# One program block for all stages, with the shared network's opening placed inside the last sequence's attention

## The chip, the cores and the metric

One NeuronCore of a Trainium2 chip runs the whole kernel. The metric is device microseconds (us) of one execution. Engines are named as in the profile: PE is TensorE (PEld its weight loads), DVE is VectorE, ACT is ScalarE, POOL is GpSimd, SP is SyncE, which only issues DMAs here.

## The reference, cut to what matters

The input x has 16 sequences of 512 tokens with 256 features. Two layers run one after the other:

```python
x = x + layernorm(attention(layernorm(x)))
x = x + layernorm(ffn(layernorm(x)))
```

The attention has 16 heads of 16 features and a causal window of 128 tokens, a small attention over 64 pooled latents, a sigmoid gate that mixes the two, and an output projection. The ffn is a mixture of experts: a router picks 2 of 8 experts (256 to 352 to 256) for each of the 8192 tokens, and a shared network (256 to 704 to 256, silu(gate) times up, then down) is applied to every token; the two are added. All matrix products are in fp32, made of three products of fp32r parts (a high part, and a low part that is the value less its high part).

## The kernel before

The work is four stages, each in a `nc.Block()` of its own (lines 317, 1496, 1910, 2170). At a block's end all five engines meet at a barrier before the next one starts. Inside a block each engine has its own hand-written order, and semaphores alone tie the engines together.

**Attention** (L317 to L1290). 16 sequences go through a software pipeline. An iteration `body(i)` has 16 positions `u`; in it run the scores, exps, selects and weighings of sequence i, the projections of i+1 (`nxt`), the norm of i+2 (`after`), the gate, mixing and output projection of i-1 (`prev`), and the residual and second norm of i-2 (`before`). Iterations 14 to 17 are unrolled; in 16 and 17 no scores are left, only the tail of sequences 14 and 15: `gate_in` (L886), `gate_mix` (L905), POOL's `mix` (L474), PE's `turn_mix` (L1193), `project_out` (L1029 to L1031, L1205), `att_stats` (L922), `residual_add` (L932), `normed` (L524). The normed rows of each sequence are stored in DRAM (`store_xn2`, L357). PE's last weighing of values is L1084.

**Shared network and routing, first half** (L1496 to L1893). It starts with `wait_ge(stored, 32 * SEQS)` on every engine: the last sequence's rows have to be in DRAM. Rounds m = 0 to 7 each take a pair of sequences: item "b" (sequence 8 + m) is only routed, item "a" (sequence m) is routed and goes through the shared network. SP loads the rows (L1509) and the weights (L1523), which ACT and DVE split into high and low parts (L1618, L1778). PE turns rows (`turn_rows`, L1816), ACT copies them (L1602, L1610), DVE makes the low part (`rows_low`, L1724), PE makes the router's logits (L1833). DVE picks the two experts (`take_logits` L1678, `choose_first` L1666 to L1685, `choose_second` L1666 to L1699), PE ranks the rows within each expert (`ranks`, L1843), DVE turns the ranks into row numbers (`place`, L1707 to L1715), and POOL scatters the rows to the experts' regions (L1562, 8 indirect DMAs an item). Meanwhile PE runs six chunks n of `gate_up` (L1394 to L1396, 12 matmuls each, 512 columns) and six of `shared_down` (12 matmuls of 256 columns). POOL also splits the experts' weights, a chunk at a time (`split_chunk`, L1569, L1571), which SP loads into one staging buffer. At the end POOL writes zero rows behind every expert's rows (L1583).

**Experts** (L1910 to L2160): 136 blocks of 128 rows, in loops. Every engine first waits in `first_part_over` for all scatters.

**Shared network, second half, and the last layer norm** (L2170 to L2454): sequences 8 to 15 through the shared network, while POOL gathers the experts' results (L2226). SP, POOL, ACT and DVE wait in `second_part_over` for the last blocks' stores.

The tensors in SBUF are allocated per stage, so the stages share the memory: the second stage's tensors lie over the attention's, which is why it could not start earlier.

Of the kernel before, what the change touches and what calls it, by code (L numbers as in the profile page):

```python
# [3 lines left out]

# [113 lines left out]
def sandwich_kernel(nc, x, qkv_w, qkv_b, rq_w, rq_b, rkv_w, rkv_b, rout_w, rout_b, out_w, out_b, gl_w, gr_w,  # L118
# [4 lines left out]
    P = 128  # L123
# [28 lines left out]
    with ExitStack() as ctx:  # L152
# [8 lines left out]

        attention = ExitStack()
        with attention:
# [3 lines left out]

            wqk_h = sb("wqk_h", [P, 2, C, D], f32r)
# [28 lines left out]
            x_in = sb("x_in", [P, T, D])  # L197
            x_res = sb("x_res", [P, T, D])
            xT_h = sb("xT_h", [P, C, S], f32r)
            xT_l = sb("xT_l", [P, C, S], f32r)  # L200
            qk_h = sb("qk_h", [P, 2, S], f32r)
            qk_l = sb("qk_l", [P, 2, S], f32r)
            kS = sb("kS", [P, 2, HEADS // 2, S], f32r)
            qS = sb("qS", [P, 2, HEADS // 2, S], f32r)
            v_sb = sb("v_sb", [P, 2, T, HEADS, PAD])
            row_max = sb("row_max", [P, G, HG, T])
            maxT = sb("maxT", [HG * T, G, P], f32r)
            prob = sb("prob", [P, SLOTS, HG, WIN])
# [72 lines left out]

            units = [(g, b) for g in range(G) for b in range(T)]
# [34 lines left out]
            with nc.Block() as block:  # L317

                @block.sync
                def _(sp):  # L320
                    sp.wait_ge(zeroed, 2)
                    with nc.allow_non_contiguous_dma(reason="512 biases, once"):
                        for dst, src in loads:
                            sp.dma_start(dst, src).then_inc(weights_in, 16)

                    sp.wait_ge(split, 1)

                    def load_x(i):
                        if not isinstance(i, int) or i > 0:
                            sp.wait_ge(*front.filled(i - 1, "xT1"))  # L330
                        sp.dma_start(x_in[:, :, :], x[i].rearrange("(t p) d -> p t d", p=P)).then_inc(x_loaded, 16)

                    def spread_heads(i, buf, half):
                        if half == 0 and (not isinstance(i, int) or i > 1):
                            for hp in range(2):
                                sp.wait_ge(*keyed.all_filled(i - 1, f"T0{hp}"))
                        tiles = slice(half * HEADS // 4, (half + 1) * HEADS // 4)
                        for j, name, dst, high, low in ((1, "k", kS, (0, 2), 1), (0, "q", qS, (0, 1), 2)):
                            sp.wait_ge((qh_ready, kh_ready)[j], HALVES * i + half + 1)
                            for term in high:  # L340
                                for par in range(2):
                                    r = par * PAIR + term * HD
                                    sp.dma_start(dst[r:r + HD, buf, tiles, :].bitcast(f32),
                                                 qk_h[par:P:2, j, :].bitcast(f32)).then_inc(spread[half], 16)
                            sp.wait_ge(*front.read(i, f"{name}{half}"))
                            for par in range(2):
                                r = par * PAIR + low * HD
                                sp.dma_start(dst[r:r + HD, buf, tiles, :].bitcast(f32),
                                             qk_l[par:P:2, j, :].bitcast(f32)).then_inc(spread[half], 16)

                    def store_x1(i):
                        sp.wait_ge(x1_ready, i + 1)
                        sp.dma_start(x1_dram[i].rearrange("(t p) d -> p t d", p=P), x_res[:, :, :]).then_inc(stored, 16)
# [937 lines left out]

        ffn = ExitStack()
        with ffn:
# [1184 lines left out]
```

## Time and profile before

| | us |
|---|---|
| median of 3 runs (2261.13 to 2278.64) | 2269.33 |
| the profiled execution, its own time | 2272.69 |
| its span | 2270.9 |

How it is read: the rows below are of one execution. Times in them count from the span's start. "[8.00 <-POOL rem L474]" behind a row says how long the engine sat idle before it, and what ended that. By the page, attention takes the span up to about 1015, its tail and the start of the shared network up to 1056, the first half of the shared network up to 1379, the experts from 1405 to 1942, and the rest is the second half.

### The profile page before, as it was taken

Reading aid. Unit: us, or ns where it says so; the run is one execution under the profiler, and the core shown is the slowest. Engines: PE = TensorE matmul, PEld = TensorE weight load, DVE = VectorE, ACT = ScalarE, POOL = GpSimd, SP = SyncE. Lnnn points to the kernel's source line nnn. Section 1 sums busy time; section 2 is a strip of 40 time slices with the busy share of each in tenths; the row PEclk is TensorE's granted clock in tenths of the full one; section 3 lists DMA queues with packets and bytes.
Section 4 is the critical chain, followed back from the end, with each engine's and each line's share of the span. In section 5 each row is a group of like instructions: output and inputs, shape, how many; then the busy total and the mean of one; then the engine's idle time right before and its main releaser. Section 6 shows DMA issues by size and latency. Waiting matters only on the chain. (4 is left out here: it accounts for less than half of the span.)

```text
span 2270.9 us, 44434 instructions
## 1 busy us (share of the span) xinstructions
PE 1902.0 (84%) x13138; PEld 1498.6 (66%) x13139; DVE 1269.7 (56%) x3150; ACT 1005.1 (44%) x2314; POOL 796.4 (35%) x947
## 2 busy tenths in 40 slices
PE   0898988898889899865898894999999999677885
PEld 0555655565556565544777783899999999466764
DVE  3667878776877777753434444333333333265655
ACT  0366666565666566543222221443444444233343
POOL 2144544444544444442535544000000000534653
PEclk9899999998999999876888886999999999788988
DMA  2745555454555555215323322122222222425553
GB/s 39 103 72 90 99 94 99 88 91 81 102 88 94 95 95 85 57 57 176 122 94 102 116 80 95 63 67 69 67 69 67 69 67 65 153 72 186 179 172 104
DMA packets 183447, 214.69 MB, mean 95 GB/s; under 512 B 28450, under 2 KB 149667, under 8 KB 183267
## 3 DMA queue, kind: packets, MB, share of 16 engines
q1 hardware_dynamic: 169394, 177.20, 34.6%
q0 software_dynamic: 12720, 34.75, 4.7%
q8 instruction: 91, 1.49, 0.3%
q10 hardware_dynamic: 1152, 0.52, 0.1%
q14 instruction: 90, 0.73, 0.1%
HBM read 92.66 MB, written 68.81 MB: 71 GB/s over the span
## 5 line engine op out<-in xcount | busy, mean ns | idle before, releaser
L443 POOL TENSOR_SCALAR_AFFINE_SELECT prob<-prob 128x512 f32<-128x512 f32 x256 | 171.5, 670 | 498.0 <-ACT prob L550 496.8
L2226 POOL DMA_INDIRECT f_y<-yg_scratch,index_all x128 | 131.2, 1025 | 588.1 <-DVE index_all L2318 550.4
L550 ACT ACTIVATE prob<-bank 128x512 f32<-128x512 f32 (+1 forms) x512 | 249.1, 538 | 136.3 <-PE bank L1071 124.2
L2005 DVE TENSOR_TENSOR b_h<-b_h,bank 128x352 f32<-128x352 f32 x136 | 70.9, 522 | 335.7 <-ACT b_h L1956 335.7
L824 DVE COPY_PREDICATED bank<-from_prev,bank 128x512 f32<-128x512 int32 x192 | 133.1, 693 | 184.0 <-PE bank L1049 156.4
L2061 PE MATMUL bank<-wgu_h,bxT_h 128*128 x544 | 190.6, 350 | 17.7 <-DVE bxT_l L2000 6.8
L827 DVE TENSOR_REDUCE row_max<-bank 128x4 f32<-128x512 f32 x256 | 177.1, 692 | 23.5 <-PE bank L1049 14.4
L2063 PE MATMUL bank<-wgu_h,bxT_l 128*128 x544 | 176.4, 324 | 0.0
L2062 PE MATMUL bank<-wgu_l,bxT_h 128*128 x544 | 175.7, 323 | 0.0
L1956 ACT ACTIVATE b_h<-bank 128x352 f32<-128x352 f32 x136 | 63.3, 466 | 251.6 <-PE bank L2063 251.6
L1084 PE MATMUL bank<-prob,v_sb 128*32 128x256 f32 (+1 forms) x2048 | 156.9, 380 | 18.7 <-ACT pvT L557 18.5
L1049 PE MATMUL bank<-kS,qS 48*128 48x256 f32 (+1 forms) x1024 | 130.8, 335 | 24.6 <-issue 12.3
L1049 PEld LDWEIGHTS bank<-kS,qS 48*128 48x128 f32 x1024 | 80.5, 195 | 103.9 <-issue 68.4
L2061 PEld LDWEIGHTS bank<-wgu_h,bxT_h 128*128 128x128 f32 x544 | 102.9, 189 | 43.3 <-issue 38.6
L447 POOL TENSOR_SCALAR_AFFINE_SELECT prob<-prob 128x512 f32<-128x512 f32 x192 | 131.1, 683 | 0.0
L2082 PE MATMUL bank<-wd_h,bhT_h 128*128 (+1 forms) x408 | 126.0, 309 | 0.7 <-ACT b_y L1967 0.7
L1394 PE MATMUL bank<-sT_h,ws_h 128*128 128x512 f32 (+1 forms) x192 | 85.2, 444 | 47.1 <-DVE s_f L1441 38.0
L1071 PE MATMUL bank<-qS,kS 49*128 49x256 f32 (+1 forms) x1024 | 109.9, 293 | 8.1 <-ACT prob L550 6.5
L2083 PE MATMUL bank<-wd_l,bhT_h 128*128 (+1 forms) x408 | 114.4, 280 | 0.0
L2084 PE MATMUL bank<-wd_h,bhT_l 128*128 (+1 forms) x408 | 114.2, 280 | 0.0
L1562 POOL DMA_INDIRECT xg_scratch<-arena,pos x64 | 62.5, 976 | 135.1 <-DVE pos L1715 117.9
L2062 PEld LDWEIGHTS bank<-wgu_l,bxT_h 128*128 128x128 f32 x544 | 103.6, 190 | 0.0
(325 smaller groups left out, 5358.1 us busy)
## 6 DMA issues: line engine op xcount, KB each, us to landing
bx<-xg_scratch SPq DMA_DIRECT2D x136, 128.0 KB, 2.0
yg_scratch<-b_y SPq DMA_DIRECT2D x136, 128.0 KB, 1.7
kS<-qk_h SPq DMA_DIRECT2D x128, 128.0 KB, 3.8
qS<-qk_h SPq DMA_DIRECT2D x128, 128.0 KB, 6.4
x_in<-in_L_attn_x_dram SPq DMA_DIRECT2D x16, 512.0 KB, 6.2
kS<-qk_l SPq DMA_DIRECT2D x64, 128.0 KB, 5.4
qS<-qk_l SPq DMA_DIRECT2D x64, 128.0 KB, 7.6
x_res<-in_L_attn_x_dram SPq DMA_DIRECT2D x16, 512.0 KB, 5.3
```

The lines of the kernel that those rows point to most:

```text
L443: op = e.affine_select(out=own, in_=own, compare_op=ALU.is_gt, fill=0.0, base=0, pattern=[[0, HG], [1, P]], channel_multiplier=-1)
L447: op = e.affine_select(out=after, in_=after, compare_op=ALU.is_gt, fill=0.0, base=0, pattern=[[0, HG], [-P, P]], channel_multiplier=P + 1)
L550: e.activation(prob[:, u % SLOTS, 2 * hp:2 * hp + 2, 0:w], src[:, :, 0:w], ACT.Exp, scale=SCALE).then_inc(keyed.frees[hp], 1)
L824: e.copy_predicated(out=own, mask=from_prev[:, :].bitcast(i32).unsqueeze(1).to_broadcast([P, HG, P]), data=prev).then_inc(score_merged, 1)
L827: e.tensor_reduce(row_max[:, g, :, b], own, AX.X, ALU.max).then_inc(score_free, 1)
L1049: op = e.matmul(SB[:, par, hh * WIN + lo:(hh + 1) * WIN], qS[rows, buf, tile, b * P:(b + 1) * P], kS[rows, buf, tile, k0:k0 + w], start=(b ...
L1084: op = e.matmul(PV[h * PAD:(h + 1) * PAD, b * P:b * P + w], v_sb[:, buf, b, g * HG + h, :], prob[:, u % SLOTS, 2 * (h % 2) + h // 2, 0:w], ...
L2061: e.matmul(out_, xh, wh, start=(c == 0), stop=False)
L2062: e.matmul(out_, xh, wl, start=False, stop=False)
L2063: op = e.matmul(out_, xl, wh, start=False, stop=(c == C - 1))
L2082: e.matmul(out_, hh, wh, start=(n == 0), stop=False)
L2226: e.indirect_dma_start(out=f_y[:, u, k, t, :], out_offset=None, in_=yg_dram, in_offset=bass.IndirectOffsetOnAxis(ap=index_all[:, T * s + t ...
```

## The change

All stages run in one `nc.Block()`, so the three inner barriers are gone; the waits on semaphores at the start of the third and the fourth stage stay. SBUF is laid out by hand: the attention's biggest tensors (kS, qS, v_sb, prob, qk, xT, x_in) now come first in memory, and the second stage's tensors are placed over those of them that are free earliest (`ws_h` over one buffer of kS, the raw shared weights over qS). The opening of the shared network is then spread over the attention's unrolled iterations:

- SP, in iteration 15, once PE has begun on the scores of sequence 15: the four gate and up pieces and the router's weights. After iteration 15, once `prob_used` says that the last weighing is done: the rows of the first two pairs and the six down pieces, ahead of iteration 16's stores.
- ACT makes the high parts of the four pieces at u = 8 to 11 of iteration 15, `rows_copy("b")` at u = 7 of iteration 16, the six down pieces' high parts, `rows_copy("a")` and `rows_high` at u = 9, the first silu at u = 15.
- DVE, in iteration 16: four low parts and the constants (u = 3), `take_logits` ahead of `gate_mix` (u = 10), `choose_first` (11), `rows_low` (12), the first `hidden` and six low parts (15). After it, sequence 15's residual and norm are interleaved with the first round's work.
- PE, in iteration 16: both `turn_rows` and the first logits at u = 7, `gate_up` n = 0 at u = 13, ahead of `project_out` of sequence 15; then `gate_up` n = 1, ranks, logits "a", and from n = 2 the order of before.
- POOL makes the constants in iteration 16; in round 0 scatter "b" now stands ahead of the first `split_chunk`. The first expert chunk and the down weights of the experts are loaded by SP after the final `stored` wait.
- The first round's turned rows and logits go to PSUM banks 0 to 3 (`small_bank`) in place of 6 and 7.

```diff
+        reserve("whole_program", LONG)
+        wd_h = sb("wd_h", [P, FCE, E, D], f32r)
 ...
+            kS = sb("kS", [P, 2, HEADS // 2, S], f32r)
+            qS = sb("qS", [P, 2, HEADS // 2, S], f32r)
+            v_sb = sb("v_sb", [P, 2, T, HEADS, PAD])
 ...
+            def small_bank(name, m):
+                opening = {"xT0b": 0, "lgb": 0, "xT1b": 1, "xT0a": 2, "xT1a": 3}
+                return psum[opening[name]] if m == 0 and name in opening else SM[small.bank(name)]
 ...
+            def shared_high_part(act, n):
+                _, full, hi, _ = shared_pieces[n]
+                if n in (0, 2 * C):
+                    act.wait_ge(piece_in[n > 0], 16 * (2 * C if n == 0 else FCS))
+                if n == 2 * C:
+                    act.wait_ge(prob_used, UNITS * SEQS)
+                nc.scalar.activation(hi, full, ACT.Copy).then_inc(shared_high, 1)
+
+            def shared_low_part(dve, n):
+                _, full, hi, lo = shared_pieces[n]
+                if n == 0:
+                    dve.wait_ge(prob_used, UNITS * SEQS)
+                dve.wait_ge(shared_high, n + 1)
+                nc.vector.tensor_tensor(lo, full, hi.bitcast(f32), ALU.subtract).then_inc(shared_split, 1)
 ...
-            with nc.Block() as block:
+            block = program.enter_context(nc.Block())
 ...
-                    for i in range(SEQS - 2, SEQS + 2):
+                body(SEQS - 2, 0)
+                for par in range(2):
+                    sp.wait_ge(*keyed.all_filled(SEQS - 1, f"T0{par}"))
+                for src, full, _, _ in shared_pieces[:2 * C]:
+                    sp.dma_start(full, src).then_inc(piece_in[0], 16)
 ...
+                body(SEQS - 1, 1)
+                sp.wait_ge(prob_used, UNITS * SEQS)
+                load_rows(sp, "b", 0)
+                load_rows(sp, "a", 0)
+                for src, full, _, _ in shared_pieces[2 * C:]:
+                    sp.dma_start(full, src).then_inc(piece_in[1], 16)
+                load_rows(sp, "b", 1)
+                load_rows(sp, "a", 1)
+                for i in range(SEQS, SEQS + 2):
                         body(i, i % 2)
                     sp.wait_ge(stored, 32 * SEQS)
 ...
+                        if at(i, SEQS) and u == 3:
+                            constants()
 ...
+                        if at(i, SEQS) and u == 7:
+                            rows_copy(act, "b", 0)
+                        if at(i, SEQS - 1) and 8 <= u < 8 + 2 * C:
+                            shared_high_part(act, u - 8)
 ...
+                        if at(i, SEQS) and u == 9:
+                            for n in range(2 * C, SHARED):
+                                shared_high_part(act, n)
+                            rows_copy(act, "a", 0)
+                            rows_high(act, 0)
 ...
+                        if at(i, SEQS) and u == 15:
+                            gate_silu(act, 0, 0, h_f)
 ...
+                keep_att(SEQS - 1, 1)
+                hidden_high(act, 0, 0, h_f, h_h)
+                for n in (1, 2, 3):
+                    first_chunk(act, 0, n)
+                normed(2, SEQS - 1, x_res, (0, 1))
+                first_chunk(act, 0, 4)
+                normed(2, SEQS - 1, x_res, (2, 3))
 ...
+                        if at(i, SEQS) and u == 3:
+                            for n in range(2 * C):
+                                shared_low_part(dve, n)
+                            routing_constants(dve)
 ...
+                        if at(i, SEQS) and u == 10:
+                            take_logits(dve, "b", 0)
                             if u == 10 and live(prev):
                                 gate_mix(prev, 0)
                                 gate_mix(prev, 1)
+                        if at(i, SEQS) and u == 11:
+                            choose_first(dve, "b", 0)
 ...
+                        if at(i, SEQS) and u == 12:
+                            rows_low(dve, 0)
 ...
+                        if at(i, SEQS) and u == 15:
+                            hidden(dve, 0, 0, h_f)
+                            for n in range(2 * C, SHARED):
+                                shared_low_part(dve, n)
 ...
+                att_stats(SEQS - 1, 1)
+                hidden_low(dve, 0, 0, h_f, h_h, h_l)
+                choose_second(dve, "b", 0)
+                hidden(dve, 0, 1, h_f)
+                hidden_low(dve, 0, 1, h_f, h_h, h_l)
+                place(dve, "b", 0)
+                take_logits(dve, "a", 0)
+                residual_add(SEQS - 1, (0, 1, 2, 3))
+                hidden(dve, 0, 2, h_f)
+                choose_first(dve, "a", 0)
+                hidden_low(dve, 0, 2, h_f, h_h, h_l)
+                residual_stats(SEQS - 1, (0, 1, 2, 3))
+                residual_scale()
+                hidden(dve, 0, 3, h_f)
+                choose_second(dve, "a", 0)
+                hidden_low(dve, 0, 3, h_f, h_h, h_l)
+                shifts(2, SEQS - 1)
 ...
+                        if at(i, SEQS) and u == 7:
+                            pe.wait_ge(score_free, UNITS * SEQS)
+                            turn_rows(pe, "b", 0)
+                            pe.wait_ge(router_in, 16 * C)
+                            logits(pe, "b", 0)
+                            turn_rows(pe, "a", 0)
 ...
+                        if at(i, SEQS) and u == 13:
+                            pe.wait_ge(shared_split, 2 * C)
+                            for c in range(C):
+                                pe.wait_ge(*small.read(0, f"xT{c}a"))
+                            gate_up(pe, 0, 0, rT_h, rT_l)
 ...
+                gate_up(pe, 0, 1, rT_h, rT_l)
+                for p in range(2):
+                    pe.wait_ge(*front.read(SEQS - 1, f"out{p}"))
 ...
-                with nc.Block() as block:
                     @block.sync
                     def _(sp):
-                        sp.wait_ge(stored, 32 * SEQS)
 ...
                         for m in range(HALF):
+                        if m > 0:
                             split_chunk(2 * m)
                             scatter("b", m)
+                        if m == 0:
+                            split_chunk(0)
                             split_chunk(2 * m + 1)
                             scatter("a", m)
 ...
                         for m in range(HALF):
+                        if m == 1:
+                            dve.wait_ge(stored, 32 * SEQS)
 ...
+        program.close()
```

## Rows read from the trace of the kernel before

**Rows 1.** The page: its first line and the line of busy times

```profile
span 2270.9 us, 44434 instructions
PE 1902.0 (84%) x13138; PEld 1498.6 (66%) x13139; DVE 1269.7 (56%) x3150; ACT 1005.1 (44%) x2314; POOL 796.4 (35%) x947
```

**Rows 2.** A window: us; busy us (instructions) of PE, PEld, DVE, ACT, POOL; PEclk, DMA, GB/s

```profile
1000.00:1056.00 56.00, 18.26 (x84) 16.78 (x84) 26.75 (x91) 16.02 (x31) 9.40 (x15) 0.57 0.40 125
```

**Rows 3.** Timeline, PE: start, us, engine, line, op, tiles, count, idle before

```profile
993.13 1.29 PE L1084 MATMUL bank<-prob,v_sb 128*32 128x256 f32 x24
...
1007.72 1.12 PE L1193 MATMUL bank<-ident,rem 128*128 128x128 f32 x4 [8.00 <-POOL rem L474]
...
1015.50 0.28 PE L1205 MATMUL bank<-bias_o,ones_r 128*128 128x256 f32 x1
...
1035.44 1.94 PE L1816 MATMUL bank<-ident,arena 128*128 128x128 f32 x8 [19.67 <-DMA arena<-xn_scratch]
...
1042.12 1.94 PE L1816 MATMUL bank<-ident,rows 128*128 128x128 f32 x8 [0.44 <-DVE rt L1678]
...
1056.19 0.79 PE L1394 MATMUL bank<-rT_h,ws_h 128*128 128x512 f32 x1 [6.15 <-DVE wsd_l L1778]
...
1061.48 0.47 PE L1843 MATMUL bank<-rt,before 128*128 128x32 f32 x2
...
1065.11 0.40 PE L1394 MATMUL bank<-rT_h,ws_h 128*128 128x512 f32 x1
```

**Rows 4.** The timeline of DVE in the same stretch

```profile
1000.25 0.22 DVE L886 TENSOR_SCALAR gate_s<-loc 128x64 f32<-128x64 f32 x1 [1.98 <-ACT rem L583]
...
1004.71 0.69 DVE L905 TENSOR_TENSOR loc<-loc,gate_s 128x512 f32<-128x512 f32 x1
...
1041.78 0.19 DVE L1678 COPY rt<-bank 128x32 f32<-128x32 f32 x1 [10.11 <-PE bank L1833]
...
1045.65 1.29 DVE L1724 TENSOR_TENSOR rT_l<-bank,rT_h 128x512 fp32r<-128x512 f32 x2 [2.33 <-ACT rT_h L1610]
...
1046.85 0.17 DVE L1666 TENSOR_REDUCE rt<-rt 128x4 f32<-128x32 f32 x1
...
1050.85 3.29 DVE L1778 TENSOR_TENSOR ws_l<-wd_l,ws_h 128x704 fp32r<-128x704 f32 x4
```

**Rows 5.** The timeline of ACT in the same stretch

```profile
1024.35 2.07 ACT L524 ACTIVATE x_res<-x_res,shift_x,rstd 128x256 f32<-128x256 f32 x4 [7.94 <-DVE shift_x L814]
...
1045.54 2.84 ACT L1618 ACTIVATE ws_h<-wd_l 128x704 fp32r<-128x704 f32 x4
...
1048.26 1.94 ACT L1618 ACTIVATE wsd_h<-wd_l 128x256 fp32r<-128x256 f32 x6
```

**Rows 6.** The timeline of SP's DMA issues in the same stretch

```profile
1026.45 0.37 SPq L357 DMA_DIRECT2D xn_scratch<-x_res  x1
...
1030.86 0.58 SPq L1509 DMA_DIRECT2D arena<-xn_scratch  x1
```

**Rows 7.** Timelines of POOL, SP and PE: the first scatter "a", a row load, its use

```profile
1080.79 1.00 POOL L1562 DMA_INDIRECT xg_scratch<-rows,pos  x1 [2.10 <-DVE pos L1715]
...
1092.46 0.38 SPq L1509 DMA_DIRECT2D rows<-xn_scratch  x1
...
1124.51 1.03 PE L1816 MATMUL bank<-ident,rows 128*128 128x128 f32 x8
```

**Rows 8.** Timelines of POOL and SP where the experts begin

```profile
1397.06 0.97 POOL L1583 DMA_INDIRECT xg_scratch<-arena,spare  x1 [0.30 <-issue]
...
1403.29 0.36 SPq L1918 DMA_DIRECT2D bx<-xg_scratch  x1
```

**Rows 9.** Timelines of POOL, ACT and PE in the last stage's first round

```profile
1988.59 0.96 POOL L2226 DMA_INDIRECT f_y<-yg_scratch,index_all  x1 [0.30 <-issue]
...
1993.06 0.60 ACT L1425 ACTIVATE s_f<-bank 128x512 f32<-128x512 f32 x1 [27.82 <-remote]
...
1994.95 0.58 PE L1394 MATMUL bank<-wsd_h,s_h 128*128 128x256 f32 x1 [13.95 <-DVE s_l L1446]
```

More of the change, by code:

```diff
@@ L3 @@
 from contextlib import ExitStack
+from math import prod
 class Steps:
@@ new lines, in sandwich_kernel @@
+        line = sb("line", [1, 3, NBLK])
+        cum_i = sb("cum_i", [P, E], i32)
+        LONG = words(ws_h, oh_all, pos_all, index_all, ws_l, table, lg_all, weight, member, counts, moved_by, grid_i, numbers,
+            iota_i, spare_rows, cum, wd_l, wsd_h, wsd_l, rows_a)
+        SHORT = words(arena, rT_h, rT_l, h_f, h_h, h_l, rt, rt1, pos, pos_f, wr, before, all_ones, base, base_p, falling)
+        phase.close()
+        reserve("whole_program", LONG)
+        wd_h = sb("wd_h", [P, FCE, E, D], f32r)
@@ new lines, in logits @@
+            def logits(pe, kind, m):
+                if m >= HALF:
+                    return
+                name = f"lg{kind}"
+                for c in range(C):
+                    if kind == "a":
+                        pe.wait_ge(xh2_ready, C * m + c + 1)
+                    else:
+                        pe.wait_ge(*small.read(m, f"xT{c}b"))
+                reached(pe, *small.drained(m, name))
+                for t in range(T):
+                    for c in range(C):
+                        op = nc.tensor.matmul(small_bank(name, m)[:, t * E:(t + 1) * E], rF[:, c, t * P:(t + 1) * P], wr[:, c, :],
+                                      start=(c == 0), stop=(c == C - 1))
+                op.then_inc(small.full(name), 1)
@@ new lines, in _, with ranks, count @@
+                @block.tensor
+                def _(pe):
+                    e = nc.tensor
+                    def ranks(kind, m):
+                        name = f"rk{kind}"
+                        pe.wait_ge(member_ready, item_of(kind, m) + 1)
+                        reached(pe, *small.drained(m, name))
+                        out_ = SM[small.bank(name)][:, 0:T * E]
+                        e.matmul(out_, before[:, :], rt[:, 6, :, :].rearrange("p t x -> p (t x)"), start=True, stop=False)
+                        e.matmul(out_, all_ones[:, :], rt[:, 7, :, :].rearrange("p t x -> p (t x)"), start=False, stop=True
+                                 ).then_inc(small.full(name), 1)
+                    def count():
+                        pe.wait_ge(*small.read(HALF - 1, "lga"))
+                        e.matmul(SM[0][:, 0:E], all_ones[:, :], member[:, :], start=True, stop=True).then_inc(counted, 1)
+                    for m in range(HALF):
+                        if m > 0:
```

3423 lines of the change are left out of this document (1690 added, 1733 removed).

## The prediction

> **What bounds the kernel now.** I read the page's busy line first: PE works 84% of the span [rows 1], so what can be won is mostly time in which PE stands still or waits for others. The table of windows shows where that is: between 1000 and 1056 PE works 18.26 of 56 us, at a granted clock of 0.57 [rows 2]. The timelines of that stretch say why. PE's last weighing of attention ends at 993.13 + 1.29 = 994.4, its last output projection at 1015.50 + 0.28 = 1015.8 [rows 3]. Then a serial tail: DVE's sums, ACT's normed rows from 1024.35 [rows 5], the store issued at 1026.45, and the first load of the next stage at 1030.86 [rows 6]. PE gets rows at 1035.44 and starts `gate_up` at 1056.19, held by the split of the last weight piece [rows 3]. The next gate_up chunks follow, and n = 2 starts at 1065.11 [rows 3]. From there on the order before and after is the same, so **the start of `gate_up` n = 2 is my anchor**: what moves it moves all that follows, as long as no new wait opens.
>
> **The change, part by part.** Times of after are estimates on before's scale.
>
> *Iteration 15.* ACT gets four high parts, 2.84 us [rows 5], among its exps; DVE and PE get nothing. POOL and PE wait for ACT's exps there. The end of weighing moves by 0 (all in ACT's gaps) to 2.84; I take half, 1.4: 995.8. SP's early loads read weights only, and what is behind them on SP's queue, the stores of sequence 13, waits for DVE and ACT anyway: nothing.
>
> *SP after iteration 15.* The row loads start at 995.8; from issue to PE's turn it took 1035.44 - 1030.86 = 4.6 [rows 3, 6], so 1000.4. PE becomes free when its idle time before turn_mix began, 1007.72 - 8.00 = 999.7 [rows 3], plus 1.4: 1001.1. The load is hidden. The ten early DMAs sit ahead of sequence 14's store of x1 on SP's queue; nobody reads that until the last stage, and the next write over it comes ten us later: nothing.
>
> *The first item, in PE's gap of 8 us.* From the turn to DVE's copy of the logits took 1041.78 - 1035.44 = 6.3 [rows 3, 4]: 1007.4. `gate_mix` is queued behind that copy. It started at 1004.71 [rows 4]; with the 1.4, and about 1.5 for DVE's four low parts (3.29 [rows 4]) and constants, partly in its idle 1.98 before `gate_in` [rows 4], it would come at 1007.6. So the two meet, and mixing is 2.9 late: POOL's mix, and PE's turn_mix at 1007.72 + 2.9 = 1010.6.
>
> *gate_up n = 0.* It needs the rows' low parts: 1045.65 + 1.29 - 1042.12 = 4.8 from the second turn [rows 3, 4], which now starts at 1007.4; ACT has the six down pieces, 1.94 [rows 5], ahead: 1014.1. PE's queue holds `project_out` behind it. n = 0 took 1061.48 - 1056.19 = 5.3 at the lower clock level, 1.2 GHz (the window's mean is 0.57 [rows 2]) [rows 3]. turn_mix to the end of project_out took 1015.8 - 1007.7 = 8.1 [rows 3]: 1010.6 + 8.1 + 5.3 = 1024.0. n = 1 hides in what follows.
>
> *To n = 2.* DVE must still do sequence 15's statistics, the low part of n = 0 (together about 2.8 behind ACT's copy) and choose_second, 1050.85 - 1046.85 = 4.0 [rows 4]: 1030.8. Ranks and logits "a" then take PE about 3.7, from the 6.3 above less one turn (1.94 [rows 3]) and ranks' 0.7: 1034.5. Against 1065.11 **30.6 us are saved**. The bounds: 24, if each wait adds a little and ACT's 2.84 counts whole; 36, if PE reaches its upper level early (ranks and n = 1 took 3.6 there, 1061.48 to 1065.11 [rows 3]) and DVE's steps fit.
>
> *What is late next.* n = 2 starts on a PE that has waited, at the lower level: 1 us, between 0 and 2.4 (5.3 less 2.9, the 3.6 above without ranks' 0.7). Sequence 15's residual and norm run on DVE and ACT between the chunks, where PE's turn of rows and waits cover them; the last `stored` comes at about 1057 (n = 3 done near 1044, nine us of steps, 4.4 from store issue to load issue [rows 6]). Only then does SP load the first expert chunk, the experts' down weights and the second chunk, and POOL's scatter "a" of round 0 is queued behind both splits. Before, it began at 1080.79, 15.7 after the anchor [rows 3, 7]. Now two chunk loads of 4.6 or more, with 2.8 MB queued ahead of the second, and the splits put it at about 1078, 43.5 after the anchor: 28 later against the pace. Who waits: the load of rows behind that scatter, issued at 1092.46 and used at 1124.51 [rows 7], a slack of 32 less 4.6 of landing, 27.4. So the slack is just used up. I take 2 us, between 0 and 10; one round later POOL has caught up.
>
> *The barriers.* Where the experts begin, POOL's last scatter ends at 1397.06 + 0.97 = 1398.0, SP's first block load is issued at 1403.29 [rows 8]: 5.3 us, in which the zero rows land, which stays awaited. 1 us saved, between 0 and 3. The same before the last stage: 1, between 0 and 2, since the wait for the last stores stays.
>
> *Instruction supply.* In the last stage's first round ACT stands still for 27.82 us, released by nothing that the trace knows, and goes on at 1993.06; PE loses 13.95 by it. POOL's burst of gathers ends at 1988.59 + 0.96 [rows 9]. The instructions in the stall are the same before and after, so I leave it in place. The Trainium skill ("Runtime: NRT & Kernel Launch", Instruction fetch mechanics) says that crossing a block of instructions costs one tail-bump that is mostly hidden, and that a taken branch out of the two resident pages stalls for a fetch; by the first half the stall is no matter of fetching and stays, by the second it could move when the program's blocks are merged. The trace doesn't agree with "mostly hidden" if the 27.82 are a fetch; it can't say that they are.
>
> *Other edits.* Tensors in other places of SBUF and round 0's rows in other banks: I know no row that a place changes, nothing.
>
> **Sum.** 30.6 - 1 - 2 + 1 + 1 = 29.6, say 30. The profiled execution took 2272.69, so it would take 2242.7; the median of the runs stands 3.4 below that execution, so **2239**. Own range of this case: 2226 to 2251.
>
> **Rivals.**
>
> *B, the tail takes it back.* The opening is packed into the queues that carry attention's tail: gate_up ahead of project_out, logits ahead of gate_mix, scatter "a" behind splits that wait for the last store. If the interleaving costs its bound of 6 and scatter "a" its 10, 14 are left: 2255. For it: the slack of 27.4 against 28 [rows 7]. Against it: POOL idles often in the rounds, as its wait of 2.10 before scatter "a" hints.
>
> *C, the stall of the last stage moves.* With fewer instructions ahead, the spot where ACT stood still falls elsewhere, behind the gathers or into a wait. PE gets 13.95 back at least, 27.82 at most [rows 9], less what POOL's gathers then limit; 19 more: 2220. For it: nothing in the program explains the stop at that instruction, and it ended 3.5 us after POOL's burst. This is what the skill's rule on branches and sequential fetch (same page and section) would allow.
>
> *D, it does not start earlier.* Some wait still ties the opening to the last store; then only the barriers go: 2267. The order in the diff shows none.
>
> *E, slower.* The same kind of stop, 27.82 us [rows 9], appears in two new places, where POOL's bursts of scatters (eight an item) meet ACT or DVE in the rounds of the first half. One such stop leaves 2 us of the gain; two give 2239 + 55.6 = 2295. It decides from the second stop on. Against it: in before eight rounds ran with sixteen bursts at known waits.
>
> **How the numbers follow.** Chances: forecast 0.45, B 0.18, C 0.25, D 0.05, E 0.07. A measurement tells about 1% (22.7 us) from no change: faster is below 2246.6. That takes 0.38 of the forecast's 0.45, all of C and a little of B: 0.66. Slower is E and a rest: 0.08. The same: 0.26. The range 2213 to 2259 leaves out E and D (0.12) and the tails of B and C (0.08).
>
> **What would show it.** Right: gate_up n = 0 stands before L1205's last row on PE, n = 2 starts at 1029 to 1041; the window 1000 to 1056 has PE at 35 us or more; gate_mix starts near 1007.6. Scatter "a" of round 0 at about 1078, and PE's second-round turn of rows "a" waits under 5 us for a DMA. The experts' first load comes 29 to 33 us before 1403.29. ACT's stop near 1963 still some 28 us. Wrong: n = 2 later than 1041 (B), no stop in the last stage (C), new stops "<-remote" above 10 us in the rounds (E), or the attention loop longer by more than 3 us per ten sequences, which I priced at nothing.

## The result and the profile after

Median of six executions of the changed kernel: **2229.38 us** (2225.64 to 2249.0), beside 2268.76 of six of the kernel before (2256.36 to 2278.64). The ratio is 0.9884, with a 95% interval of 0.9835 to 0.9932. The forecast was 2239, in a range of 2213 to 2259. The profiled execution of after took 2246.15 us, 26.5 less than that of before; it was granted a mean clock of 0.916. The four executions granted 0.924 to 0.928 took 2226 to 2230.

Two landmarks are used throughout. *V* is the start of the last matmul that weighs values in attention (994.1 in before, 1006.3 in after); E is the experts' first gate matmul (1407.3 and 1378.8). The stretch in which PE worked 18.26 of 56 us at a clock of 0.57 [rows 2] is now this, in the table of windows (stretch, length, busy time and count by engine, clock, share of the DMA engines, GB/s):

```profile
1000.00:1056.00 56.00, 44.93 (x256) 36.66 (x255) 38.71 (x139) 23.98 (x49) 12.81 (x19) 0.79 0.34 110
```

PE's own timeline (start, length, line and operands, in brackets the idle time before and what ended it) shows the first item inside attention's end:

```profile
1005.32 1.29 PE L1580 MATMUL bank<-prob,v_sb 128*32 128x256 f32 x24
1011.75 1.04 PE L562 MATMUL bank<-ident,arena 128*128 128x128 f32 x8
1013.73 1.92 PE L579 MATMUL bank<-wr,arena 128*128 128x8 f32 x16 [0.94 <-ACT arena L594]
1017.69 1.94 PE L562 MATMUL bank<-ident,rows_a 128*128 128x128 f32 x8 [2.04 <-DVE rt L636]
1020.46 1.12 PE L1689 MATMUL bank<-ident,rem 128*128 128x128 f32 x4 [0.83 <-POOL rem L905]
...
1024.61 0.77 PE L489 MATMUL bank<-rT_h,ws_h 128*128 128x512 f32 x1 [1.09 <-DVE rT_l L651]
...
1038.71 0.41 PE L1989 MATMUL bank<-rt,before 128*128 128x32 f32 x2 [2.50 <-DVE member L667]
1039.18 2.48 PE L579 MATMUL bank<-wr,arena 128*128 128x8 f32 x16
1041.51 0.77 PE L489 MATMUL bank<-rT_h,ws_h 128*128 128x512 f32 x1
```

L562 turns the rows, L579 makes the logits, L489 at 1024.61 is `gate_up` n = 0, and at 1041.51 the anchor, n = 2. It stood at 1065.11 [rows 3], V + 71.0; it is now at V + 35.2. V itself is 12.2 us later than before.

What answers to [rows 7]: the expert chunks that POOL must split ahead of scatter "a" come late, and PE then waits for rows behind that scatter. From POOL's, SP's and PE's timelines:

```profile
1073.91 0.77 POOL L1867 CAST wgu_h<-chunk_in 128x704 fp32r<-128x704 f32 x1 [10.20 <-DMA chunk_in<-in_L_ffn_w_up_dram]
1087.38 0.79 POOL L1867 CAST wgu_h<-chunk_in 128x704 fp32r<-128x704 f32 x1 [10.93 <-DMA chunk_in<-in_L_ffn_w_up_dram]
1090.10 1.01 POOL L1860 DMA_INDIRECT xg_scratch<-rows_a,pos  x1 [0.17 <-issue]
...
1101.43 0.38 SPq L728 DMA_DIRECT2D rows_a<-xn_scratch  x1
...
1105.74 1.97 PE L562 MATMUL bank<-ident,rows_a 128*128 128x128 f32 x8 [8.03 <-DMA rows_a<-xn_scratch]
```

And what answers to [rows 8, 9], the experts' first load and ACT's long stop:

```profile
1374.61 4.08 SPq L2054 DMA_DIRECT2D bx<-xg_scratch  x4
...
1965.47 0.60 ACT L520 ACTIVATE s_f<-bank 128x512 f32<-128x512 f32 x1 [26.96 <-remote]
```

### The profile page after: what moved, and what is told of

Its sections match the earlier page's. It is cut to its first block, busy times and chain, and to the rows that moved or that the text cites. A ratio compares the mean times of both kernels' runs of the same rounds, so it can differ in the third digit from the quotient of the medians.

```text
span 2244.4 us, 44405 instructions
## 1 busy us (share of the span) xinstructions
PE 1911.8 (85%) x13138; PEld 1504.3 (67%) x13139; DVE 1286.2 (57%) x3150; ACT 1002.6 (45%) x2314; POOL 793.0 (35%) x947
## 4 chain that ended last, share of the span: by engine, by line
PE 59%; issue 11%; DVE 10%; ACT 7%; POOL 4%; another core or an unknown queue 4%; DMA 3%; SPq 1%; ACTq 1%; POOLq 0%; DVEq 0%
PE bank L2197 5%; PE bank L2198 4%; PE bank L2199 4%; PE bank L1525 3%; PE bank L489 3%; PE bank L1580 3%; PE bank L1545 3%; PE bank L491 3%; PE bank L490 3%; ACT prob L997 3%; PE bank L1526 3%; PE bank L1527 3%; PE bank L2218 2%; PE bank L2220 2%
## 5 line engine op out<-in xcount | busy, mean ns | idle before, releaser
L1580 PE MATMUL bank<-prob,v_sb 128*32 128x256 f32 (+1 forms) x2048 | 158.9, 384 | 18.4 <-ACT pvT L1004 18.2
L1545 PE MATMUL bank<-kS,qS 48*128 48x256 f32 (+1 forms) x1024 | 131.4, 337 | 24.2 <-issue 12.2
L489 PE MATMUL bank<-sT_h,ws_h 128*128 128x512 f32 (+1 forms) x192 | 85.6, 446 | 40.9 <-issue 21.8
L2199 PEld LDWEIGHTS bank<-wgu_h,bxT_l 128*128 128x128 f32 x544 | 103.4, 190 | 0.0
```

Source lines behind the costliest of these rows:

```text
L489: e.matmul(out_, lh, rh, start=first, stop=False, skip_group_check=True)
L1545: op = e.matmul(SB[:, par, hh * WIN + lo:(hh + 1) * WIN], qS[rows, buf, tile, b * P:(b + 1) * P], kS[rows, buf, tile, k0:k0 + w], start=(b ...
L1580: op = e.matmul(PV[h * PAD:(h + 1) * PAD, b * P:b * P + w], v_sb[:, buf, b, g * HG + h, :], prob[:, u % SLOTS, 2 * (h % 2) + h // 2, 0:w], ...
L2199: op = e.matmul(out_, xl, wh, start=False, stop=(c == C - 1))
```

## The experiments

The runs fell on several chips, and that turned out to matter. On chip 13 (e0 to e3) and chip 6 (e5 to e8) the kernel before takes 2139 and 2137 us; on chip 10 (e9 to e12) 2260, as in the first comparison, whose chip isn't recorded. Each run is compared with the kernel before on its own chip, and the last two are called the slower chips below.

**e0, the changed kernel once more.** 

> The changed kernel once more, beside kernels that undo parts of it. In its profiled execution attention's last weighing began at 1005.32, in that of the kernel before at 993.13, 12.2 us earlier, and that execution was one of the two slow ones of six (2246 at a mean granted clock of 0.916, the four others 2226 to 2230 at 0.924 to 0.928). Theory: the 12.2 us are the clock that this execution was granted, and belong to no edit. Then the last weighing begins between 990 and 1008 from execution to execution, near 993 where the mean clock is 0.925 or more, and start of gate_up n = 2 follows it by 36 in any case. Rival: the new places of attention's tensors cost 12 us in the loop; then it is at 1004 to 1008 again, whatever the clock. Median 2229, 2224 to 2249.

Measured on chip 13: 2120.85, before 2138.78, ratio 0.9925 (0.9893 to 0.9957). V was at 989.3, n = 2 at V + 35.2. Over all twelve traces with the changed kernel's attention V lies between 989.3 and 1015.9, and follows one thing, how long TensorE was granted only its lower level (1.2 GHz) between 100 us and V: 95.6 us in e0, 136.5 in after, 163.8 in e1. A straight line, 952.9 + 0.386 x that time, meets all twelve V within 1.6 us. So the 12.2 us are the clock of one execution, as the theory had it. The two traces of the kernel before lie 3.1 and 4.1 above that line (99.0 us at the lower level, V 994.1; 92.2, V 992.5): attention itself seems some 3 or 4 us shorter in the changed form. No run takes that apart.

**e1, the opening put back, the single block kept.** On SP, for example:

```diff
-                sp.wait_ge(prob_used, UNITS * SEQS)
-                load_rows(sp, "b", 0)
...
                 for i in range(SEQS, SEQS + 2):
                     body(i, i % 2)
                 sp.wait_ge(stored, 32 * SEQS)
+                load_rows(sp, "b", 0)
```

> One block of instructions and the new places in SBUF stay; all work of the opening (loads and splits of weights, rows, router, gates) is put back behind attention's end, in the order of the kernel before. Theory (the gain is the overlap, the program's form is worth the barriers only): n = 2 starts 66 to 72 us after the last weighing began (before 72.0, changed 36.2), and the time is 2264, 2258 to 2269 beside 2268 of before. Rival (merging the blocks and moving the tensors gives part of it, by instruction supply or places): 2240 or less.

Measured: 2137.31, ratio 0.9986 (0.9955 to 1.0017); n = 2 at V + 67.7. (POOL's order of round 0 stays as changed here and in e2.) The program's form alone is worth nothing that can be told from zero; the gain is the overlap.

**e2, only the weights early.** The same, but the loads and splits of the shared weights stay in attention. 

> As e1, but loads and splits of the shared weights, the router's load and the routing constants stay inside attention, as in the changed kernel; rows, routing and gates wait for the last store. Theory: in before PE stood from the end of logits a near 1047 until 1056.19 for the split of the last weight piece; that goes, so n = 2 starts 57 to 62 after the last weighing and the time is 2255, 2249 to 2260. The other 25 us of the overlap then belong to the rows. Rival (the weights' split was what held PE, the rows follow anyway): n = 2 at 36 to 45 after it, 2235.

Measured: 2127.73, ratio 0.996 (0.9924 to 0.9996), n = 2 at V + 61.8. About as the theory had it: of the 32.5 us between e1 and e0 at n = 2 the weights give 5.9, the rows, routing and gates the other 26.6. Yet E - V is 338.1 in e1, 332.3 in e2 and 324.0 in e0. **Of 32.5 us at n = 2, 14.1 are left at the experts' start.** The windows of 80 us from n = 2 on (in e1 from 0.3 us behind it) and of the rest of the shared network (PE busy, clock, DMA, GB/s), first e0, then e1, say how they are lost:

```profile
1024.50:1104.50 80.00, 71.13 (x387) 0.84 0.47 146
1104.50:1289.70 185.20, 185.07 (x1143) 0.98 0.40 132
```

```profile
1083.90:1163.90 80.00, 80.00 (x499) 0.98 0.44 138
1163.90:1330.50 166.60, 166.43 (x1029) 0.98 0.38 129
```

With the opening late PE has a full queue from n = 2 on, at a clock of 0.98. With it early PE works 71 of the 80 us at 0.84 and executes 387 of the 499 matmuls that it did there. Three waits stand in that window of e0:

```profile
1021.21 0.41 PE L1989 MATMUL bank<-rt,before 128*128 128x32 f32 x2 [2.49 <-DVE member L667]
...
1038.37 0.41 PE L1989 MATMUL bank<-rt,before 128*128 128x32 f32 x2 [2.22 <-DVE member L667]
...
1086.45 1.97 PE L562 MATMUL bank<-ident,rows_a 128*128 128x128 f32 x8 [6.64 <-DMA rows_a<-xn_scratch]
```

(The first is just ahead of n = 2.) They hold 11.4 us, and the lower level of the clock 25.2 of the 80 us, where e1 has 3.4. Executions of the same code differ here: in after and in e5, whose rounds are those of the changed kernel, the lower level took 19.3 of the 80 us, and PE waited 8.03 and 8.01 us for rows "a".

**e3, `gate_up` n = 0 behind project_out.**

```diff
-                        if at(i, SEQS) and u == 13:
-                            ...
-                            gate_up(pe, 0, 0, rT_h, rT_l)
...
+                gate_up(pe, 0, 0, rT_h, rT_l)
                 gate_up(pe, 0, 1, rT_h, rT_l)
```

> The changed kernel with gate_up n = 0 moved on PE from ahead of project_out to behind it, with the gate's silu and product moved alike on ACT and DVE. Theory: n = 0 fills a gap in which PE waits for the mixed values anyway, and the chain through DVE's choose_second and PE's ranks comes 2.6 us later when it has to queue behind the late n = 0: n = 2 starts 37 to 41 after the last weighing, 2232, 2228 to 2236 for executions at a clock of 0.925. Rival (n = 0 stands in the way of attention's tail, which decides): n = 2 at 31 to 34, 2225.

Measured: 2117.01, ratio 0.9921 (0.9887 to 0.9956), n = 2 at V + 35.7, E - V 322.5. Neither: the place of n = 0 shows no cost and no gain here. My 2.6 us were wrong, because ranks "b" still wait 2.56 us for DVE's choose_second: DVE's chain sets that point, not PE's order.

**e6, scatter "a" of round 0 ahead of the splits.**

```diff
                         if m == 0:
+                            scatter("a", m)
                             split_chunk(0)
                         split_chunk(2 * m + 1)
-                        scatter("a", m)
+                        if m > 0:
+                            scatter("a", m)
```

> The changed kernel with POOL's order of round 0 altered: its scatter of rows a goes ahead of the splits of expert chunks 0 and 1, which wait for loads that can only be issued after attention's last store. In the repeat of the changed kernel PE waited 6.64 us for rows a of round 2, and the granted clock was 0.86 and 0.83 in the first two stretches of 40 us after n = 2, where it was 1.00 and 0.96 in the kernel with the late opening; from the last weighing to the experts' first matmul it took 324.0 us against 338.1, only 14.1 less, though n = 2 started 33 earlier. Theory (the late scatter takes part of the overlap back): the wait of 6.64 goes below 1 us, the dip of the clock behind it goes too, weighing to experts takes 313 to 319, and the time is 5 to 11 us below the changed kernel's in the same state, ratio to before 0.988 to 0.990. Rival (PE's low clock and DVE's waits of round 0 decide, rows a come in their shadow): 322 to 325, ratio 0.992 again. On a chip whose rounds have idle time of their own, as in the first measurement, the gain is at most 3.

Measured on chip 6: 2113.58, ratio 0.9916 (0.9884 to 0.9947). The wait is gone (0.98 is left, for rows "b"), the lower level of those 80 us is down to 12.7, and E - V to 315.3, inside the theory's 313 to 319. Counted from e0 on chip 13 that is 8.7 us less. The nearer neighbour is e5 (below), on the same chip 6 and with the changed kernel's rounds: E - V 322.3, lower level 19.3, and this wait:

```profile
1101.66 1.97 PE L562 MATMUL bank<-ident,rows_a 128*128 128x128 f32 x8 [8.01 <-DMA rows_a<-xn_scratch]
```

Counted from it e6 gains 7.0. By the ratio alone e6 is not told from e0; the trace shows it.

**e7, two of PE's items later.**

```diff
+                        if m == 0:
+                            logits(pe, "a", 0)
+                            pe.wait_ge(shared_split, SHARED)
                         ranks("b", m)
...
-                        ranks("a", m)
                         gate_up(pe, m, 4, rT_h, rT_l)
```

(ranks "a" follows in round 0.) 

> The changed kernel with two items of PE's order in round 0 altered: logits a ahead of ranks b, and ranks a behind gate_up n = 4. In the repeat of the changed kernel PE waited 2.49 us ahead of ranks b and 2.22 ahead of ranks a for DVE's choose_second. Theory (each short wait is lost in full, and lowers the clock behind it): both waits go, weighing to experts takes 316 to 321 instead of 324, the time is 3 to 8 us lower than the changed kernel's. Rival (the placing of the rows then comes later, so POOL's scatters and all rows behind them do, and PE's wait for rows a grows from 6.64 by what is saved): 323 to 326, no gain.

Measured: 2109.44, ratio 0.9902 (0.9861 to 0.9942), E - V 314.3, 9.7 us less than e0's and 8.0 less than e5's. Both waits went (a new one of 0.85 ahead of ranks "b" is left), and n = 2 came at V + 32.4. The wait for rows "a" is 8.06, above e0's 6.64, but e5, e3 and after wait 8.01 to 8.03 with the old order, so the rival's growth is not seen. Of the 8.0 us against e5, 2.8 lie ahead of n = 2; behind it PE stands idle for 2.4 us less, and the lower level lasts 5.6 us less (26.1 to 20.5 up to the end of the shared network; 19.3 to 13.7 in the first 80 us), which by the 0.386 above is some 2 us, an estimate.

**e8, both.** 

> Both of the two reorderings together, as the version that could beat both kernels. Theory (the rounds lose to the early opening 19 of its 33 us through three PE waits and the lower clock behind them): no wait of PE above 1 us between n = 2 and the end of the shared network, clock 0.93 or more in the first 80 us, weighing to experts 308 to 315 where the changed kernel takes 324, ratio to before 0.984 to 0.988. Rival (the clock stays low in these 80 us whatever PE waits for): 315 to 320, ratio 0.989 to 0.991.

Measured: 2104.29 (2098.73 to 2109.71), **ratio 0.9861 (0.9821 to 0.9902)**, the lowest on these chips: 33.1 us below the kernel before on its chip, where e0 was 17.9 below on its own. E - V 311.6, the lower level 10.2 of the 80 us, the clock 0.94. The theory's E - V, clock and ratio came, its "no wait above 1 us" did not. The two don't add up (7.0 and 8.0 us alone, 10.7 together, against e5), since a new wait opened on PE, for the rows "b" of round 2, whose load is queued on SP behind the expert chunk that POOL now splits later:

```profile
1074.90 1.65 PE L562 MATMUL bank<-ident,arena 128*128 128x128 f32 x8 [4.78 <-DMA arena<-xn_scratch]
```

**e5, the gathers of the last stage paced.**

```diff
+                                if p < 2 and k == 1 and t % 2 == 1:
+                                    gp.wait_ge(gathered[u], 16 * 2 * (t + 1))
```

> The changed kernel with the 32 gathers at the start of the last stage paced: POOL waits after every four until they have landed. In the profiled executions of before and of the changed kernel ACT stood for 27.82 and 26.96 us beside these gathers, released by nothing that the trace knows; in the repeat on another chip no such stop was there. Theory (the unbroken burst of gathers keeps ACT and PE from their next instructions): on a chip with the stop it shrinks below 10 us, and the last stage gets 10 to 20 us shorter; on one without it nothing is gained and 0 to 5 us are lost, because DVE gets its gathered rows later. Rival (the stop belongs to the place in ACT's program): it stays at 25 to 28 us where it is seen.

Measured on chip 6, where there was no stop: 2131.85, ratio 0.9984 (0.9955 to 1.0014). The last stage, from the experts' last gate matmul to the end, took 279.8 us instead of the 269.9 to 270.4 of e6, e7 and e8 on the same chip, a loss of 9.5, more than expected. What pacing does where the stop exists wasn't tried. Up to the last stage this is the changed kernel, and so the repeat of it on chip 6 from which e6 to e8 are counted.

**e9, e8 with rows ahead of chunks on SP.** In round 0 `load_rows` "b" goes ahead of expert chunk 1, and "a" ahead of chunk 2.

> e8 with SP's order of round 0 altered as well: the loads of rows b and a of round 2 go ahead of expert chunks 1 and 2, whose loads wait for POOL's splits. In e8 PE had a new wait of 4.78 us for rows b of round 2, and weighing to experts took 311.6 (changed kernel 324.0, late opening 338.1). Theory (that wait is SP's, queued behind the chunk): it goes, and weighing to experts takes 305 to 309, ratio to before 0.982 to 0.986. Rival (the rows then meet the chunks and the down weights on the DMA engines, or POOL's scatters end no earlier): 311 to 313, ratio as e8's 0.986.

Measured on chip 10: 2243.42, before 2259.79, ratio 0.9896 (0.9857 to 0.9935). PE's wait for rows "b" is gone, but E - V is 377.7, against 372.5 of the changed kernel in the first comparison; on such chips two executions of one kernel differ by more than that (e11). POOL's two scatters of round 0 now make one run of sixteen, from 1046.35 to 1066.59, and beside it ACT stands, then PE:

```profile
1058.99 1.08 ACT L971 ACTIVATE x_res<-x_res,shift_x,rstd 128x256 f32<-128x256 f32 x2
1069.08 0.59 ACT L520 ACTIVATE h_f<-bank 64x512 f32<-64x512 f32 x1 [9.00 <-remote]
```

```profile
1071.18 3.56 PE L579 MATMUL bank<-wr,arena 128*128 128x8 f32 x16 [9.35 <-DVE rT_l L651]
```

The prediction of 305 to 309 was made for a chip without such stops; neither theory could be tested.

**e10, work added to PE's waits.**

```diff
+                        if m == 0:
+                            filler(2, 5)
                         ranks("b", m)
```

(and `filler(4, 8)` ahead of ranks "a".) 

> The changed kernel with work added: 5 idle matmuls on PE ahead of ranks b of round 0 and 8 ahead of its ranks a, where PE waits 2.49 and 2.22 us for DVE; their results are overwritten and nobody reads them. In the repeat of the changed kernel the clock was at its lower level for 25.3 of the 80 us behind the start of n = 2; with those two waits gone (e7) for 11.9, and with the late opening (e1) for 3.4. Theory (a good half of what the rounds lose is the lower clock behind the waits, not the waits): with filled waits the lower level takes 15 us or less, weighing to experts 317 to 321 instead of 324.0, and the time falls by 3 to 7 though PE does more. Rival (only the waits cost, the clock is by the way): 324 to 326, time as the changed kernel's.

Measured on chip 10: 2226.93, ratio 0.9833 (0.9797 to 0.9869), E - V 361.5. It is the fastest on chip 10 although PE does more. But the theory's own sign failed: the fillers cut the first wait to 1.37 us and the second to 0.20, and still the lower level took 25.4 of the 80 us, not 15 or less. A stretch at the lower level began 1.1 us ahead of n = 2, as in after; the one that followed the second wait there (1057.4 to 1060.8) is gone, but the later ones are longer. So this doesn't show that filling a wait holds the clock up. The changed kernel itself was not run on chip 10, the interval overlaps that of the first comparison (0.9835 to 0.9932), and the E - V of two executions of the kernel before differ by 18.5 us on the slower chips (413.2, and 394.7 in e11). I leave it as inconclusive.

**e11, the kernel before, for its trace.** 

> The kernel before once more, for its trace on this chip. Theory: n = 2 starts 68 to 71 us after the last weighing, as in the first trace (71.0) and with the late opening (68); weighing to experts takes 339 to 343, near the late opening's 338.1 and far from the 413.2 of the first chip, since the rounds here have none of the short stops seen there; PE is busy for all of the rounds. Rival (the rounds of before have waits of their own that the late opening lost with its block borders or its places): 350 or more.

Measured on chip 10: 2257.47, ratio 0.9991 (0.9959 to 1.0024), n = 2 at V + 70. E - V is 394.7, since this was again a chip with the stops; what it was meant to show on a chip without them stays with e1.

**e12, e9 and e3 together.** 

> e9 with gate_up n = 0 behind project_out, as in e3, where weighing to experts took 322.5 against 324.0 although n = 2 started 0.5 later. Theory (n = 0 ahead of project_out delays attention's last store, and with it the first expert chunk; e9 no longer depends on that): no gain over e9, within 1.5 us of its weighing to experts. Rival (the last store still decides something): 2 to 4 us less than e9.

Measured: 2237.66, ratio 0.9874 (0.9826 to 0.9922), E - V 376.2 against e9's 377.7. The place of n = 0 shows no difference once more.

## Why the prediction was right, step by step

**The time.** 2229.4 against 2239, inside the forecast's own range of 2226 to 2251, on the faster side. By the ratio the gain is 26 us (15 to 37) where 30 were forecast; on chip 13 it is 16, which a forecast from one trace can't know. Part of the match is luck. The profiled execution of after ends 26.5 us earlier than that of before, and this is 35.8 (the anchor, counted from V) and 4.9 (from the anchor to E), less 12.2 (V itself), 0.7 (the experts) and 1.3 (the last stage). The forecast had 30.6 for the anchor with V's part in it, 3 lost in the rounds and 2 won at the barriers. Of the signs named beforehand, the order on PE, its 44.93 us in the window and ACT's stop came true. The wait for rows "a" did not (8.03, not under 5), the experts' first load narrowly not, and one sign of "wrong" did appear: attention was 12.2 us longer in sixteen sequences, above 3 per ten. e0 shows that this was the clock of one execution.

**Until n = 2: right mechanism, gain mis-sized low.** Counted from V, n = 2 came 35.8 us earlier (71.0 to 35.2) in after, e0 and, within half a microsecond, e3 and e10. I had 30.6 with V itself 1.4 late, so 32.0 from V, 3.8 too low. Of the parts: iteration 15's ACT parts, priced at 1.4, cost nothing that shows, as e1, which has none of them, lies on the same line of V against the clock (0.2 below it); with a scatter of up to 1.6 about that line, 1.4 isn't ruled out. gate_mix started 11.1 us after V; before it was 10.6 [rows 4], so it was 0.6 late, where I had 1.5 besides V's 1.4. The rest is DVE's: ranks "b" could start at V + 32.4, where I had choose_second end 35.3 after the weighing, since I had put attention's statistics and the low part in a row ahead of it. The bound of 36 in the text was the better number.

**Behind n = 2: the step that failed in size.** I took 1 us for the clock (0 to 2.4) and 2 for late rows (0 to 10). On chip 13 the two together took 18.4 of 32.5. From n = 2 to the end of the shared network PE needed 246.9 us in e1 and 265.2 in e0: 9.2 of the difference is PE standing idle, and the lower level lasted 32.0 us instead of 10.2, which by the 0.386 us per us of attention makes some 8, an estimate. So the term that was too small by most is the clock's, 1 where some 8 were lost. The mechanism is that of rival B: scatter "a" came 48.6 after the anchor in after (43.5 forecast), and PE waited 8.03 us for rows "a" of round 2 (under 5 forecast; 6.64 in e0). What I hadn't priced at all is that an item that starts early runs beside a DVE that is still busy with attention, so that PE, which had a full queue, now has gaps, and more of the lower clock comes with them: in e0 three of the five stretches at the lower level within those 80 us begin in one of the three waits or about 1 us behind its end, the other two behind none. I costed the clock of one chunk, not of the next 80 us. e6, e7 and e8 show it from three sides. Against e5, and with new waits counted, they took 7.2, 3.7 and 7.0 us off PE's waits; E - V fell by 7.0, 8.0 and 10.7, and the lower level of the 80 us from 19.3 to 12.7, 13.7 and 10.2 us. That the waits are what brings the clock down is argued from this, not shown: e10 filled two of them and the lower level stayed. In the first comparison these losses hardly show, since PE stood idle in the rounds there in before too (33.2 us from n = 2 to the shared network's end, 34.8 in after): E - V fell from 413.2 to 372.5, more than at the anchor. With 18.5 us between two executions of before, that single difference isn't to be read closely.

**The barriers.** Forecast 2 us together. PE stood 24.3 us ahead of the experts' first block, in before 26.8 and in e11 24.4; e1 is at 0.9986, with 1 inside its interval. Nothing that a run tells from zero. The experts' first load came 28.7 us earlier than 1403.29 [rows 8], just under the forecast's 29 to 33.

**The stop of the last stage.** Left in place, and it stayed: 26.96 us where there were 27.82 [rows 9], though much of ACT's code ahead of it changed. In e9, e10 and e12 it was 28.33, 30.49 and 28.38; in e11, the kernel before, it came as 18.70 and 10.95. Rival C would have moved it. By the Trainium skill ("Runtime: NRT & Kernel Launch", Instruction fetch mechanics) a taken branch out of the two resident pages stalls for a fetch. The traces show no fetch in this stop: from 1938.51 to 1965.47 in after, and from 1965.24 to 1993.06 in before, no packet of an instruction queue moves. ACT was waiting for a semaphore of PE (below), so "released by nothing that the trace knows" holds for the views, not for the trace. D and E did not come true: n = 2 is earlier by 35.8, no unexplained wait in the rounds of after exceeds 6.5 us, and their sum was 102.4 us there and 106.3 in before.

**Other places in SBUF.** Priced at nothing; the two traces of before lie 3 to 4 us above the changed kernels' line. If it is the places, they gave part of the gain of the medians. It stays open.

## What to carry to other kernels

Pulling work forward into another stage's tail is worth what the bottleneck engine's queue keeps of it: look not only at when the first item starts but at whether that engine then has a full queue. Here about half of what was lost again was idle time, and the other half came with the lower clock. After such a change reorder the first round for it (here the scatter ahead of the splits, the ranks behind a chunk): by the ratios (0.9925 to 0.9861, on two chips) that gave another 14 us or so on chips without the stops, 10.7 of it between V and E. And check the reordering on the chips where it will run: on chip 10, e9 and e12 (0.9896 and 0.9874) stand no lower than the changed kernel in the first comparison (0.9884), and in both PE waits some 9 us beside or just behind their one run of sixteen scatters.

## What the runs showed of the hardware

**On some chips the other engines stop beside bursts of indirect DMAs.** I counted the waits above 0.7 us on ACT, PE and DVE that the views put down to "remote" or "issue", that is to nothing they know. In the rounds, from n = 2 to the experts, they are 53 in before, with 106.3 us, in after 47 with 102.4, in e9 52 with 121.0. Every one of them overlaps a run of POOL's indirect DMAs or the 1.5 us behind it, though such runs fill only half of the time. In the last stage of before it is 32 of 32, of after 44 of 45 (the other one is 0.81 us, just behind the burst). On the chips 13 and 6 none of the eight profiled executions has such a wait in the same stages. There the rounds and the last stage are 48.5 and 69 us shorter (e0 against after: E - V 324.0 and 372.5, last stage 267.2 and 336.4), while the experts' stage, which has no such bursts, takes 528.9 and 529.2. The same burst of 32 gathers in the last stage, first in after, then in e0 (columns as above, with PE, PE's weight loads, DVE, ACT and POOL):

```profile
1920.50:1960.40 39.90, 20.79 (x79) 15.34 (x79) 9.29 (x18) 3.01 (x6) 30.44 (x32) 0.71 0.59 183
```

```profile
1854.70:1896.20 41.50, 36.79 (x188) 30.63 (x189) 27.88 (x71) 10.91 (x20) 31.98 (x32) 0.95 0.66 202
```

POOL issues the same 32 in nearly the same time, at 183 and 202 GB/s, and PE gets 79 or 188 matmuls done beside it. The stop is no matter of bandwidth, then. In e0 ACT's longest wait in that stretch is for DVE:

```profile
1875.76 0.62 ACT L526 ACTIVATE s_h<-s_f 128x512 fp32r<-128x512 f32 x1
1882.46 0.63 ACT L526 ACTIVATE s_h<-s_f 128x512 fp32r<-128x512 f32 x1 [6.08 <-DVE s_f L536]
```

**In the long stop a semaphore's update comes late.** The packed trace also holds the times of the semaphores' updates, which no view prints. ACT's long wait of before is for the semaphore that PE raises behind a `gate_up` chunk. PE's last matmul of that chunk ends at 1965.12, the update stands at 1993.04, 27.9 us later, and ACT starts 0.02 us behind it; in after it is 1936.82 and 1965.45, 28.6 us, and in e9, e10 and e12 28.2, 28.4 and 28.7. The view finds no instruction that ended near the update, and so writes "remote". In the rounds and the last stage of after, 339 of the 1321 instructions of PE, ACT and DVE that raise a semaphore have no update within 0.2 us of their end, and 336 of the 339 end in a run of indirect DMAs or up to 1.5 us behind one. In attention and among the experts of the same execution there is none, and in e0 none anywhere. For most of them the trace can't tell a late update from one that is missing from the record; in the long stop ACT's start tells that it was late.

That the bursts go with the stops, and a late update with the longest of them, is shown. That the bursts are the cause is argued, since no run on these chips left them out or spaced them; what delays the update, and why only on some chips, is open.

**The granted clock decides between executions.** Attention's end moved by 26.6 us over twelve executions of nearly the same code, 0.386 us for each us at the lower level, and no other difference of that size is seen between them. A difference of 12 us between two traces, such as the one between before and after here, says nothing of an edit until the clock's part is taken off.
